# A macaron block (FFN, causal attention, FFN) on one Trainium2 core: normalisation of two batches moved from VectorE to ScalarE, and narrow tiles' copies moved ahead

## What is computed

```python
x = x + 0.5 * ffn(layernorm(x))
x = x + attn(layernorm(x))
x = x + 0.5 * ffn(layernorm(x))

def attn(x):                     # causal, one head of 128
    Q, K, V = x @ Qw, x @ Kw, x @ Vw
    scores = einsum('bqd,bkd->bqk', Q, K) / sqrt(128) + mask
    return einsum('bqk,bkd->bqd', softmax(scores), V)

def ffn(x):                      # 16 experts of width 64, top 4, plus a shared one of 128
    hid = relu(einsum('th,eih->eti', x, W1)) ** 2
    out = einsum('eth,te->th', einsum('eti,ehi->eth', hid, W2), cw)   # cw: routing weights
    return out + relu(x @ Ws1.T) ** 2 @ Ws2.T
```

## Time and profile before

| | us |
|---|---|
| median of 3 runs | 685.28 (681.53 to 686.0) |
| the profiled execution | 686.61 |
| its span | 684.8 |
| outside the span | 1.8 |

### The profile page before, as it was taken

The page is one execution under the profiler, slowest core; times in us unless marked ns, Lnnn a source line. Parts: engine busy times, 40 slices in busy tenths (PEclk is TensorE's granted clock), DMA queues, the critical chain, the costliest instruction groups (busy, mean ns, idle before and its releaser), DMA issues.

```text
span 684.8 us, 15211 instructions
## 1 busy us (share of the span) xinstructions
PE 640.4 (94%) x3395; PEld 493.8 (72%) x3395; DVE 559.1 (82%) x2576; ACT 549.7 (80%) x1171; POOL 521.7 (76%) x411
## 2 busy tenths in 40 slices
PE   4689999999999997699998998999999999999997
PEld 3457777777777765578776886777777777777775
DVE  5888989989899897767767768779889889898863
ACT  3478879898888874778887786769888898988975
POOL 3378889899998885665655546558899998999975
PEclk9699999999999999999999999999999999999999
DMA  9866677865777650334544435886867878768782
GB/s 245 194 139 128 140 160 151 167 130 129 161 158 165 134 124 1 59 74 76 96 81 78 74 76 96 162 161 123 171 143 159 176 170 174 160 142 187 167 172 76
DMA packets 107801, 92.05 MB, mean 134 GB/s; under 512 B 59488, under 2 KB 73456, under 8 KB 107760
## 3 DMA queue, kind: packets, MB, share of 16 engines
q1 hardware_dynamic: 105552, 91.00, 63.6%
q10 hardware_dynamic: 2208, 0.59, 0.4%
HBM read 72.70 MB, written 5.24 MB: 114 GB/s over the span
## 4 chain that ended last, share of the span: by engine, by line
PE 69%; DVE 13%; ACT 6%; issue 6%; DMA 3%; POOL 2%; SPq 0%; POOLq 0%; ACTq 0%; DVEq 0%
PE psum L1373 18%; PE psum L1374 17%; PE psum L1375 17%; PE psum L1446 3%; DVE w_raw L1246 3%; DMA wb<-scratch 2%; PE psum L1404 2%; PE psum L1458 2%; DVE zn L1272 1%; PE psum L1420 1%; DVE s_sb L1100 1%; PE psum L1412 1%; PE psum L1610 1%; ACT s_sb L759 1%; PE psum L1612 1%
## 5 line engine op out<-in xcount | busy, mean ns | idle before, releaser
L452 POOL TENSOR_TENSOR shared_r<-shared,shared_r 128x512 fp32r<-128x512 f32 x256 | 326.6, 1298 | 57.7 <-ACT shared L642 55.1
L1100 DVE SCALAR_TENSOR_TENSOR s_sb<-psum,wb 128x512 f32<-128x512 f32 x256 | 175.6, 687 | 47.4 <-DMA wb<-scratch 22.4
L641 ACT ACTIVATE shared_r<-s_sb 128x512 fp32r<-128x512 f32 x256 | 160.0, 625 | 46.3 <-DVE s_sb L1100 43.0
L642 ACT ACTIVATE shared<-s_sb 128x512 f32<-128x512 f32 x288 | 177.6, 619 | 20.0 <-DVE s_sb L1100 20.0
L1373 PE MATMUL psum<-x_hi,w_hi 128*128 128x512 f32 x288 | 126.3, 439 | 1.2 <-issue 0.9
L1373 PE MATMUL psum<-shared_r,w_hi 128*128 128x512 f32 x256 | 115.6, 452 | 1.2 <-POOL shared_r L452 1.0
L1375 PE MATMUL psum<-x_hi,w_lo 128*128 128x512 f32 x288 | 114.2, 396 | 0.0
L1374 PE MATMUL psum<-x_lo,w_hi 128*128 128x512 f32 x288 | 114.0, 396 | 0.0
L1374 PE MATMUL psum<-shared_r,w_hi 128*128 128x512 f32 x256 | 101.7, 397 | 0.0
L1375 PE MATMUL psum<-shared_r,w_lo 128*128 128x512 f32 x256 | 101.0, 395 | 0.0
L544 POOL TENSOR_TENSOR shared<-s_sb,shared 128x1024 f16<-128x1024 f32 (+3 forms) x32 | 56.7, 1771 | 44.3 <-ACT shared L572 44.3
(11 more groups left out here) (170 smaller groups left out, 1372.3 us busy)
## 6 DMA issues: line engine op xcount, KB each, us to landing
wb<-scratch SPq DMA_DIRECT2D x128, 512.0 KB, 7.9
out<-x_sb SPq DMA_DIRECT2D x16, 256.0 KB, 9.9
x_sb<-in_L_attn_x SPq DMA_DIRECT2D x4, 256.0 KB, 6.2
scratch<-wT SPq DMA_DIRECT2D x32, 32.0 KB, 1.9
w_raw<-in_L_ffn_W ACTq DMA_DIRECT2D x1, 512.0 KB, 6.0
w_raw<-in_L_ffn_W SPq DMA_DIRECT2D x1, 512.0 KB, 6.6
wb<-shared SPq DMA_TRANSPOSE x32, 4.1
w_raw<-in_L_ffn_Ws ACTq DMA_DIRECT2D x1, 64.0 KB, 8.7
```

Of the source, the lines that this page charges most:

```text
L452: nc.gpsimd.tensor_tensor(g_lo[:, j % RING, :], g_f[:, j % RING, :], g_hi[:, j % RING, :].bitcast(F32), ALU.subtract).then_inc(F.glo_done, 1)
L641: nc.scalar.activation(g_hi[:, j % RING, :], s_sb[:, j % RING, :], ACT.Square)
L642: nc.scalar.activation(g_f[:, j % RING, :], s_sb[:, j % RING, :], ACT.Square).then_inc(F.sq_done, 1)
L1100: ins = nc.vector.scalar_tensor_tensor(s_, h_, 0.0, wb[:, u, c, :], ALU.max, ALU.mult)
```

## The change

It has four pieces. (1) VectorE's `normalise` is gone; the 16 tiles of batches 0 and 1 go to ScalarE's own `normalise`, two at a time, in slots 4 to 7 and 14 to 17 of the last body. ScalarE's form needs `a_shift`, so VectorE makes `shift(0)` in slot 4 and `shift(1)` in slot 13; statistics and means are moved to suit, and `mean(2)` goes from the loop to slot 17. (2) In batch 0, ScalarE's `z_hi` copies come behind the exponential, and VectorE closes the first FFN (its last residual) one slot later, behind `z_lo`. (3) In every batch TensorE transposes the narrow tiles first in slots 5 and 6, and ScalarE copies SOON[1] ahead of the exponential of slot 6. (4) ScalarE's `start_ffn` comes ahead of the normalisation and of `prob_hi` in its slot.

```diff
--- before.py
+++ after.py
@@ -772,18 +772,23 @@
                     sc.wait_ge(A.tp_done, HQ * b + SOON.index(t) + 1)
                     copy(pT[:, 0:t + 1, q0:q0 + P], tp_ps[:, 0:(t + 1) * P].rearrange("p (k q) -> p k q", q=P)).then_inc(A.pT_done, 1)
 
-                def normalise(b, half):
-                    sc.wait_ge(A.shift_done, b - 1)
+                def normalise(b, half, tiles=range(HQ)):
+                    sc.wait_ge(A.shift_done, b + 1)
                     tokens_free(sc, b, half)
-                    for t in range(half * HQ, (half + 1) * HQ):
+                    for t in (half * HQ + n for n in tiles):
                         ins = nc.scalar.activation(zn(b, half)[:, t % HQ, :], x_sb[:, b * QT + t, :], ACT.Identity, bias=a_shift[:, t:t + 1],
                                                    scale=a_rstd[:, b % UN, t:t + 1])
-                    ins.then_inc(A.zn_done[half], 1)
+                    if tiles[-1] == HQ - 1:
+                        ins.then_inc(A.zn_done[half], 1)
 
                 def begin(k):
 
                     if k == 3:
                         nc.scalar.activation(warm[:], neg_half[:], ACT.Exp)
+                    if k in (4, 5, 6, 7):
+                        normalise(0, (7 - k) // 2, range(k % 2 * 2, k % 2 * 2 + 2))
+                    if k in (14, 15, 16, 17):
+                        normalise(1, (k - 14) // 2, range(k % 2 * 2, k % 2 * 2 + 2))
                     if k == 8:
                         z_hi_copy(0, 1, misc_ps)
                     if k == 11:
@@ -804,22 +809,26 @@
                                 pT_copy(b - 1, SOON[3])
                             if b > 0 and s == 4:
                                 uT_copy(b - 1, 1)
-                            if b > 0 and s == 6:
-                                uT_copy(b - 1, 0)
-                            if b + 1 < B and s in (0, 2):
+                            if s == 6:
+                                if b > 0:
+                                    uT_copy(b - 1, 0)
+                                pT_copy(b, SOON[1])
+                            if b + 1 < B and s in (0, 2) and b > 0:
                                 z_hi_copy(b + 1, s // 2, prep_ps)
                             exp(b, s)
-                            if s in (5, 6):
-                                pT_copy(b, SOON[s - 5])
+                            if b == 0 and s in (0, 2):
+                                z_hi_copy(1, s // 2, prep_ps)
+                            if s == 5:
+                                pT_copy(b, SOON[0])
                             if b + 1 < B and s in (4, 6):
                                 q_hi_copy(b + 1, (6 - s) // 2, prep_ps)
+                            start_ffn((b - (B - 2)) * QT + s)
                             if b + 2 < B and s == 4:
                                 normalise(b + 2, 1)
                             if b + 2 < B and s == 6:
                                 normalise(b + 2, 0)
                             if s % 2 == 1:
                                 prob_hi(b, ORDER[s - 1])
-                            start_ffn((b - (B - 2)) * QT + s)
 
                     pT_copy(B - 1, SOON[2])
                     pT_copy(B - 1, SOON[3])
@@ -1264,15 +1273,6 @@
                     nc.vector.scalar_tensor_tensor(a_shift, a_mv[b % UN][:, :, 0], -1.0, a_rstd[:, b % UN], ALU.mult,
                                                    ALU.mult).then_inc(A.shift_done, 1)
 
-                def normalise(b, half):
-                    v.wait_ge(A.rstd_done, b + 1)
-                    tokens_free(v, b, half)
-                    for t in range(HQ):
-                        tile = half * HQ + t
-                        ins = nc.vector.tensor_scalar(zn(b, half)[:, t, :], x_sb[:, b * QT + tile, :],
-                                                      a_mv[b % UN][:, tile, 0:1], a_rstd[:, b % UN, tile:tile + 1], ALU.subtract, ALU.mult)
-                    ins.then_inc(A.zn_done[half], 1)
-
                 def finish(b, half):
 
                     v.wait_ge(A.exp_done, QT * b + QT - half)
@@ -1294,42 +1294,42 @@
                         stats(0, 1)
                     if k == 2:
                         mean(0)
-                    if k in (3, 4):
-                        stats(1, k - 3)
-                    if k == 5:
-                        normalise(0, 1)
+                    if k == 4:
+                        shift(0)
+                    if k in (3, 5):
+                        stats(1, (k - 3) // 2)
                     if k == 6:
                         mean(1)
-                    if k == 7:
-                        normalise(0, 0)
                     if k == 9:
                         z_lo_part(0, 1, misc_ps)
-                    if k == 10:
-                        normalise(1, 0)
                     if k == 12:
                         z_lo_part(0, 0, u_ps)
-                        normalise(1, 1)
+                    if k == 13:
+                        shift(1)
+                        stats(2, 0)
                     if k == 14:
                         q_lo_part(0, 1, misc_ps)
-                    if k in (13, 15):
-                        stats(2, (k - 13) // 2)
+                        stats(2, 1)
                     if k == 16:
                         q_lo_part(0, 0, u_ps)
+                    if k == 17:
+                        mean(2)
 
                 def run():
                     for b in range(B):
                         for s in range(QT):
                             row_max(b, s)
-                            if b == 0 and s == 0:
+                            if b == 0 and s == 1:
+                                z_lo_part(1, 0, prep_ps)
                                 close_ffn()
                                 v.wait_ge(FF[0].res_done, NG)
-                            if b + 1 < B and s in (0, 2):
+                            if b + 1 < B and s in (0, 2) and (b, s) != (0, 0):
                                 z_lo_part(b + 1, s // 2, prep_ps)
                             if b + 1 < B and s in (5, 7):
                                 q_lo_part(b + 1, (7 - s) // 2, prep_ps)
-                            if b + 2 < B and s == 1:
+                            if 0 < b < B - 2 and s == 1:
                                 mean(b + 2)
-                            if b + 3 < B and s in (1, 4):
+                            if b + 3 < B and s in ((1, 4) if b > 0 else (3, 5)):
                                 stats(b + 3, s // 4)
                             if b + 2 < B and s == 3:
                                 shift(b + 2)
@@ -1669,14 +1669,14 @@
                             if s == 4 and new:
                                 q_product(b + 1, 1, prep_ps)
                             if s == 5:
+                                prob_transpose(b, SOON[0])
                                 if b > 0:
                                     mix(b - 1)
-                                prob_transpose(b, SOON[0])
                             if s == 6:
+                                prob_transpose(b, SOON[1])
                                 if new:
                                     pe.wait_ge(A.qlo_done[1], b + 2)
                                     q_product(b + 1, 0, prep_ps)
-                                prob_transpose(b, SOON[1])
                                 if b > 0:
                                     values(b - 1, 1)
                             if s == 7:
```

## The result

| | before | changed |
|---|---|---|
| median, us | 684.33 (681.53 to 686.0, 4 runs) | 673.17 (672.18 to 673.56, 4 runs) |
| ratio to before | | 0.9838, 95% interval 0.9808 to 0.9868 |
| span of the profiled execution | 684.8 | 671.3 |
| mean granted clock | 0.982 | 0.996 |

The change makes the kernel 1.6% faster: 11.2 us by the medians, 9 to 13 by the interval. The spans differ by 13.5 us, and that is too much to put down to the change. A part of it lies ahead of everything that was edited. The last transposes of `oT` in front of the edited slots start at 243.25 in TensorE's timeline of before,

A forecast was written before the change was run, and what follows sets the result against it. The FFN-to-attention handover was taken to hold most of the loss, with 9.30 us of VectorE normalisations in its chain. Gains 7.2 + 3.0 = 10.2 us put the median near 675.1, stated as 676.0 for short waits; range 671.5 to 681.5.

The forecast's parts named there:

- (a): Rival, chance 0.13: ScalarE becomes the bound at the handover, with the 16 normalisations ahead of its squares' copies; 679.8 us.
- (b): Rival, chance 0.09: in the attention loop a new wait in slot 6 replaces slot 7's; 678.1 to 679.5 us.
- Part 1: FFN-to-attention handover: the 16 normalisations on ScalarE start the first score product at 265.7 instead of 271.37, gain 5.7.
- The queue sum: ScalarE's work from 250.2 to `q_hi` of half 1: squares 8.84, normalisations 3.08, copies 1.5; 13.4, ending at 263.6.
- Batch 1's eight behind `q_hi`: ScalarE's queue: 3.1 us of normalisations beside the first score product, delaying half 0's `q_hi` by 1.5 and the first exponential.
- Part 2: Batch 0's order: full clock saves 1.3, first exponential 7.8 earlier, pair product 7.2 earlier; 7.2 together with the moved normalisations.
- Part 3: Batches 1 to 7, narrow tiles first: gains sum to 3.8, taken as 3.0, bounds -1.4 and 6.1.
- The even share of 4.4: Batches 1 to 7: seven of TensorE's nine waits for narrow tiles' copies, an even share of 5.7 us.
- The waits for narrow copies: Sign of being right: TensorE's waits under 3 us in all, with new ones of 0.3 to 0.7 in slot 6.
- (c): Rival, chance 0.05: TensorE idles early at the handover and runs at the lower clock; about 686 to 695 us.
- (d): Rival, chance 0.05: the second FFN's weights' DMA or VectorE slots take the gain; about 3 left, 682 us.
- The stretching: VectorE's normalisations, 332 to 1450 ns with one shape, are stretched by exclusion with GpSimd; this does not follow them to ScalarE.

The follow-up runs named there:

- x1: Kernel before with only the 16 normalisations moved to ScalarE in the new slots, without the early `mean(2)` and the loop's orders: 678.8 us, 0.74% faster.
- x2: Kernel before with only the loop's orders, narrow tiles first and `start_ffn` earlier (pieces 3 and 4): 678.8 us, 0.81% faster.
- x9: Changed kernel with, in batch 0 alone, the `q` product of slot 6 ahead of the narrow tile's transposes again: last score product 185.23 against 185.14.
- x4: Kernel before with piece 4 alone, `start_ffn` ahead of the normalisations and `prob_hi` on ScalarE: 681.3 us, 0.29% faster.
- x8: Kernel before with piece 3 alone, narrow tiles' transposes and copies first: 0.15% faster, 0.9 us by its median, interval reaching over no change.
- x3: Changed kernel with the 16 normalisations back on VectorE, in pairs in the same new slots: the slots there give 0.05%, nothing measurable.
- x7: Changed kernel with batch 1's eight normalisations on VectorE in the same new slots, batch 0's on ScalarE: 678.34 us, 4 to 5 us slower than the changed kernel.
- x6: Changed kernel with `mean(2)` put back into slot 1 of batch 0: third score product 0.64 earlier, no gain in time.
- x5: Changed kernel with piece 2 undone, `z_hi` ahead of the exponential and the FFN's last residual in its old slot: same time as the changed kernel.
- x11: Changed kernel with four normalisations (batch 0, half 0) back on VectorE in slot 8: 673.64 us against 673.17.
- x12: Changed kernel with both four normalisations (batch 0, half 0) back on VectorE and batch 0's `q` product first in slot 6: 673.5 us, ratio 0.9826.

## Why the prediction was right, and where its steps were off

The forecast of 676.0 us (range 671.5 to 681.5) is met by 673.17, and its mechanism is the one that the runs show: the normalisations off VectorE (x1) and the loop's orders (x2) give some 5 us each. The measured gain of 11.2 is above the 10.2 of the sum, and the 0.9 that was then taken off for short waits was not needed. The range was wide enough to hold rivals (a) and (b) too, so it is the runs and not the number that tell them apart. Its fast end was also taken lower than its own terms give (685.3 - 7.2 - 6 = 672.1). Step by step:

- **Part 1, the start of the first score product.** It started at 28.12 before (271.37 less 243.25) and at 22.79 here:

```profile
264.14 0.39 PE L1373 MATMUL psum<-z_hi,x_hi 128*128 128x512 f32 x1
```

  (TensorE's timeline.) A gain of 5.3 where 5.7 was forecast. The queue sum, with its allowance of 0.8, put `q_hi` of half 1 at 264.4, which is 21.15 by the mark; it started at 21.11. ScalarE's timeline:

```profile
247.09 0.62 ACT L641 ACTIVATE shared_r<-s_sb 128x512 fp32r<-128x512 f32 x1
...
261.40 0.63 ACT L641 ACTIVATE shared_r<-s_sb 128x512 fp32r<-128x512 f32 x1 [0.81 <-DVE s_sb L1111]
...
262.46 0.58 ACT L572 ACTIVATE x_hi<-psum 128x512 fp32r<-128x512 f32 x1
```

  That it is so close is in part luck. Between the first and the last of these rows ScalarE has nine pairs of squares and a single one, not eight and one: 9 x 1.04 + 0.52 + 3.08 (normalisations) + 1.43 (copies) + 0.9 of waiting = 15.3, not 14.2. The pair that I left out, 1.04, is offset by the start: I held the gate at 249.79 for fixed by the DMA, and it was not; by the mark it stands at 5.72 here where it stood at 6.54, and in x9, where it waited 1.15 for the DMA, the score product was not later. The wait for gate 17, allowed at 0.8, was 0.81. The 0.3 that are missing are TensorE's own: it had matmuls of the FFN until 264.14 without a gap. And 0.3 to 0.8 of the 5.3 are in the profile of before alone: x2, x4 and x8, with the same program there, start the product at 27.3 to 27.8, not at 28.12. What the forecast did not see is that other slots on VectorE would have given two thirds of this mark (x3 starts the product at 24.18), though nothing of the time.
- **Batch 1's eight behind `q_hi`.** They were said to lie beside the first score product, and do. What that is worth is seen in x3 and x7: on VectorE they hold the first row maximum, and x7, the clean case, is 4 to 5 us slower.
- **Part 2.** The first score product ran at full clock, as forecast; before, its matmuls had 2.70 us at 0.50. That this 1.3 came with the change is luck, though: in x2 and x8 TensorE waits as long ahead of this product (2.46 and 2.45, before 2.46), and it runs in 1.48. The third came 7.9 earlier (forecast 7.8). The first pair product stands at 42.73, where it stood at 48.80, 6.1 earlier and not 7.2. What the sum lacked is the clock, which falls to 0.50 in slot 6. The waiting there is not longer, 1.72 against 0.87 and 1.02 before. But from these transposes to the first pair product the changed kernel takes 3.03 us, and x2, with the same matmuls at 1.00, 1.64. TensorE's timelines, changed (its transposes start at 281.05, in the row above) and then x2:

```profile
284.08 0.29 PE L1610 MATMUL psum<-wb,zn 128*128 128x256 f16 x1
```

```profile
287.44 0.52 PE L1587 MATMUL psum<-ident,shared 128*128 128x128 f32 x3 [1.72 <-ACT w_raw L572]
289.08 0.27 PE L1612 MATMUL psum<-wb,zn 128*128 128x256 f16 x1
```

  In the profile of before the second low stretch (291 to 296) lies behind the pair product instead, so that 7.6 are there again at batch 1's first score product. `mean(2)` ahead of the row maximum was charged 0.75 and costs 0.64 (x6), but the order in batch 0 as a whole is worth nothing in the time (x5).
- **Part 3.** Forecast 3.8 by the sum, taken as 3.0; batches 1 to 7 gained 3.6. (The even share of 4.4 was too high: the two waits of batch 0 were 1.9 of the 5.7, and 3.8 were left.) Batches 1, 2 and 5 gained 0.1 each (0.2 forecast), batch 6 0.6 (0.6), batches 3 and 4 1.5 and 1.4 (1.0 each); batch 7 lost 0.3 where a gain of 0.6 was forecast. The wait of slot 7 became one of slot 6, as said. TensorE's timeline in batch 2 (before, 0.61):

```profile
320.53 0.52 PE L1585 MATMUL psum<-ident,shared 128*128 128x128 f32 x3 [0.67 <-ACT w_raw L572]
```

  The waits for narrow copies, forecast under 3 us in all, came to 3.9, 1.72 of them in batch 0. The row of the waits, 264 to 450 us:

```profile
PE psum L1585 <- ACT w_raw L572: 3.9, 5, 1.7
```

- **Rivals.** (a), ScalarE as the bound, was right in part as a mechanism and too dear in its price: ScalarE's queue holds the first score product back (x11), by 0.75 us. (b), that the new wait takes the place of the old, describes batches 1, 2 and 5, and x8, piece 3 alone, has only 0.15%; but batches 3, 4 and 6 gain 0.4 to 0.6 each in x8, and 1.5, 1.4 and 0.6 with piece 4. (c), a slower kernel by the clock, did not come: the stretch from 250 to 272 ran at 1.00. The Trainium skill ("TensorE: Matmul & The Clock Gate", on the clock gate) has activity releasing the array's clock. The runs here do not bear out what the forecast drew from it, that a denser stretch keeps the high level: from 250 to 272 us x2, x3 and x8, with 17.58 to 18.03 us of work in 22, ran at 1.00 like the changed kernel with its 20.16, and batch 0 ran at 0.93 in the changed kernel and at 1.00 in x2. (d), a later stage that takes it, is visible only in small: the stretch behind the last score product took 244.8 to 245.3 in the two kernels, and between 244.5 and 246.5 in the others, with 245.7 and more in x5 and x8 to x12.
- **The stretching.** That the stretching of VectorE's normalisations (332 to 1450 ns) would not follow them to ScalarE is borne out. Line L779 in the changed kernel from 240 to 300 us (shortest, median, longest):

```profile
L779 ACT ACTIVATE zn<-x_sb,w_raw x24: 478/482/492, 248.1 to 299.2; 128x128 f32<-128x128 f32 x24
```

  On VectorE in x3 the same sixteen still range from 321 to 1397 ns, as expected of it. The two `shift` that were added took 1.09 and 0.69 us, where the shortest of the four in this stretch took 0.15. That is 1.5 us more for the two; about one was said to be possible. What held them no run shows.

```profile
L1273 DVE SCALAR_TENSOR_TENSOR w_raw<-w_raw x4: 150/798/1092, 245.8 to 293.9; 128x8 f32<-128x8 f32 x4
```

What stays open: why the transposing transfer lands 1.6 us later in three of the kernels (a packet of instructions beside it was seen, not tried); why the new slots, worth 3 us at the first score product on VectorE, leave nothing in the time; and what decides where the low clock falls.

## What to carry to other kernels

When work is moved to another engine, add up the queue that receives it from the oldest instruction still waiting in it; and compare two executions from a mark on the engine that is hardly ever idle (TensorE here), not from an instruction that waits for a DMA. Try the new places in the order on the old engine too, and judge by the time of the whole kernel: here the slots alone gave half of the gain at the first score product and none at the end. Find out which part of the moved work had to go (here batch 1's, which held the first row maximum). And gains of one or two microseconds at a mark in the middle are not gains of the kernel: x9, x11 and x12 each reached a mark earlier by 0.75 to 2.1 us, and none was measurably faster. Look at the granted clock of both executions before such a difference is put down to an edit: most of x9's 1.5 us was the clock.

## What the runs showed of the hardware

- The low level of TensorE's clock falls at different places in kernels, and in stretches, that are alike. By windows of 1 us the granted clock in batch 0 was under 1.00 from 271 to 275 and from 291 to 296 before; from 271 to 275 and 285 to 289 in x1; from 280 to 285 in the changed kernel; nowhere in x2. From 275 to 279 it was low in x12. It was low in the opening (0.80 to 0.82 in the first 30 us) of before, x1 and x8, whose first 30 us have the same code as the others', at 1.00; that cost nothing that shows (the first square at 32.52 before, 32.55 in the changed kernel). A stretch in which the matmuls are what others wait for costs what they take longer: 1.3 us at the first score product, 0.9 to 1.1 at the third, 1.4 ahead of the first pair product, 1.27 at 42 to 47 us. Two profiles can therefore differ by 2 to 4 us without any doing of the edit; x8's ten runs spread over 7.4, from 679.77 to 687.13.
- VectorE's normalisation of one 128x128 tile, of one shape, takes 0.32 to 1.45 us over the eight kernels that have it, in x11 and x12 from the same slot 1.53 and 2.13 for four; ScalarE's takes 0.48 to 0.55 in all fourteen.
- The transposing transfer of one wide tile, 1312 packets each time, landed 3.4 us after its issue in eleven kernels and 5.0 to 5.1 in three.
